# q, k, v of the first attention, rotated keys and latents of the second: from float32 matmuls to three float32r products of high and low parts

## The reference

```
x  = x + layernorm(attention1(layernorm(x)))          # "layer 1"
x1 = layernorm(x)
# attention1: 16 heads of 32
qkv = x @ w_qkv ; q, k = rotary(q), rotary(k)
out = softmax(causal(q k^T / sqrt(32))) v @ w_o
# "layer 2": latent attention on rmsnorm(x1) * ln1_w, then x = x + layernorm(h + experts(h))
kv_d = x @ kv_d_w ; q_d = x @ q_d_w                   # the latents, 128 wide each
k = [kv_d @ k_u_w, rotary(x @ rope_k_w)]              # plain keys, rotated keys
q = [q_d @ q_u_w, rotary(q_d @ rope_q_w)] ; v = kv_d @ v_u_w
h = x1 + softmax(causal(q k^T / sqrt(32))) v @ o_w
```

## Time and profile before

| | |
|---|---|
| median of three runs | 2467.84 us (2466.0 to 2468.34) |
| the profiled execution, its own time | 2468.37 us |
| its span in the trace | 2466.6 us |
| TensorE busy | 2212.0 us, 90% |
| VectorE / ScalarE / GpSimd busy | 61% / 44% / 43% |
| granted TensorE clock, mean | 0.956 |
| attention part (64 head groups) | from the start to about 1715 us |

### The profile page before, as it was taken

The page is one execution under the profiler, slowest core; times in us unless marked ns, Lnnn a source line. Parts: engine busy times, 40 slices in busy tenths (PEclk is TensorE's granted clock), DMA queues, the critical chain, the costliest instruction groups (busy, mean ns, idle before and its releaser), DMA issues. The chain is left out here.

```text
span 2466.6 us, 38146 instructions
## 1 busy us (share of the span) xinstructions
PE 2212.0 (90%) x12944; PEld 1515.4 (61%) x12944; DVE 1511.5 (61%) x4192; ACT 1083.1 (44%) x2214; POOL 1064.4 (43%) x1092
## 2 busy tenths in 40 slices
PE   6898989989898998988899898898498899999994
PEld 5665555656555566655656665464266688888873
DVE  3656667665676765667666566765366556655657
ACT  1334554333555433454533344454233255555543
POOL 1455454444554443456353355544145233333322
PEclk9999999999999999999999999997699899999996
DMA  5443545434455443444544444343438588788796
GB/s 176 113 121 103 145 141 161 121 111 113 121 146 167 122 134 104 119 131 139 163 121 127 129 115 132 98 106 103 169 129 290 209 217 198 184 214 200 185 274 228
DMA packets 221391, 374.83 MB, mean 152 GB/s; under 512 B 24847, under 2 KB 95375, under 8 KB 218383
## 3 DMA queue, kind: packets, MB, share of 16 engines
q1 hardware_dynamic: 157454, 272.69, 37.8%
q0 software_dynamic: 17792, 39.99, 8.4%
q10 hardware_dynamic: 45952, 59.71, 6.7%
HBM read 126.88 MB, written 144.24 MB: 110 GB/s over the span
## 5 line engine op out<-in xcount | busy, mean ns | idle before, releaser
L646 ACT ACTIVATE probs<-scoresT 128x512 f32<-128x512 f32 (+3 forms) x1024 | 417.8, 436 | 551.5 <-PE scoresT L1031 545.9
L827 DVE CUSTOM_DVE_ANT_0 unused<-score,mask 128x128 bf16<-128x128 f32 (+3 forms) x1024 | 465.8, 485 | 267.9 <-PE score L1008 254.0
L1008 PE MATMUL score<-stacks 96*128 96x256 f32 (+2 forms) x1024 | 390.6, 425 | 49.7 <-DVE rowmax L827 47.9
L1031 PE MATMUL scoresT<-stacks 97*128 97x256 f32 (+2 forms) x1024 | 406.2, 432 | 22.0 <-ACT probs L646 10.1
L579 POOL TENSOR_TENSOR probs<-probs 128x1536 f32<-128x1536 f32 (+1 forms) x128 | 373.2, 2916 | 46.4 <-PE out_ps L1045 38.4
L1008 PEld LDWEIGHTS score<-stacks 96*128 96x128 f32 x1024 | 182.3, 193 | 250.6 <-issue 179.9
L840 DVE RECIPROCAL total<-total 128x128 f32<-128x128 f32 x256 | 232.7, 932 | 95.4 <-ACT whole L657 90.0
L568 POOL TENSOR_SCALAR_AFFINE_SELECT probs<-probs 128x512 f32<-128x512 f32 x256 | 164.2, 641 | 291.7 <-ACT probs L646 291.6
L938 PE MATMUL middle<-wqkv,XT 128*128 128x128 f32 x2048 | 270.1, 280 | 7.1 <-ACT XT L613 6.1
L938 PEld LDWEIGHTS middle<-wqkv,XT 128*128 128x128 f32 x2048 | 260.4, 195 | 22.1 <-issue 8.4
L1668 POOL DMA_INDIRECT h_summed<-y,goal x88 | 141.7, 1610 | 292.3 <-ACT y L1764 272.2
(11 more groups left out here) (185 smaller groups left out, 3815.0 us busy)
## 6 DMA issues: line engine op xcount, KB each, us to landing
stacks<-parts SPq DMA_DIRECT2D x768, 128.0 KB, 2.4
x_slots<-mask ACTq DMA_DIRECT2D x56, 1032.0 KB, 4.7
xr<-x_slots SPq DMA_DIRECT2D x22, 1032.0 KB
raw<-in_gates SPq DMA_DIRECT2D x24, 512.0 KB
raw<-in_ups SPq DMA_DIRECT2D x24, 512.0 KB
raw<-in_downs SPq DMA_DIRECT2D x24, 512.0 KB
normed<-in_L_attn_x SPq DMA_DIRECT2D x8, 1024.0 KB, 8.7
rows<-in_L_attn_x SPq DMA_DIRECT2D x8, 1024.0 KB, 5.6
```

What stands on the lines that cost most here:

```text
L646: act.activation(probs[j][:, h, 0:width], scoresT[:, u % ST_BANKS, first:first + width], ACT.Exp, scale=SCALE).then_inc(exp_done, 1)
L827: ins = dve.tensor_tensor_reduce(unused[:, t, 0:width], score.bank(name)[:, first:first + width], mask[:, T - width:T], 1.0, MASKED, ALU.a ...
L1008: ins = pe.matmul(score.bank(name)[:, first:first + width], heads[0:ROWMAX, 0, h, t * P:(t + 1) * P], heads[0:ROWMAX, 1, h, 0:width], star ...
L1031: pe.matmul(scoresT[:, u % ST_BANKS, 0:T - first], heads[0:ROWMAX + 1, 1, h, j * P:(j + 1) * P], heads[0:ROWMAX + 1, 0, h, first:T], start ...
```

## The change

Every operand of P (layer 1), V (layer 1), KR and LAT is split into a high part (float32r, a copy by ScalarE) and a low part (what is left, by VectorE). Instead of one float32 matmul, `three` sums high by high, high by low and low by high, each a float32r matmul. To have 256 moving columns, P makes q and k of a head group side by side: step P(n, 0) is row tiles 0 and 1 of both, P(n, 1) row tiles 2 and 3. So both transposes, of q and of k, now wait for both rotations. V comes in four parts (two row tiles by half of the columns), KR in two (two row tiles, all heads).

The weights are split once at the start (steps WQ, WV for layer 1, WS for layer 2); the raw weights are put into buffers not yet in use. The buffer `wturn` holds the split weights of V for layer 1 or of KR and LAT for layer 2: both versions, 2 MB each, are stored to DRAM (WK) and read back when the layer turns (WT, seven times). `wo` holds one layer's weights and is loaded again at each turn (WO). The input of an attention, transposed, is `xh` and `xl`: its PSUM bank is free only after VectorE has written `xl`.

V parts 2 and 3 of an attention are made in its own g = 1, parts 0 and 1 in g = 2 and 3 of the one before. KR stands wholly in g = 2. `columns_of` is adapted, with XT at four times its columns; `S_AT` starts at 0.27 instead of 0.24.

The diff, cut:

```
-S_AT = (0.24, 0.055)
+S_AT = (0.27, 0.055)
...
     if g == 1:
+        early = quarters("V", c, 2) + quarters("V", c, 3)
+        if starts and start_layer == 1 and core_of(c)[1] == 0:
+            early += [("WT", p)]
...
-            steps = own[:4] + quarters("Y", f, 3) + own[4:] + [("HS", f)]
+            steps = early + quarters("Y", f, 3) + own + [("HS", f)]
...
     if step == "P":
-        return (4 * CT * P, 4 * P)[core_of(which[0] // NG)[1]]
+        return (12 * P, 4 * P)[core_of(which[0] // NG)[1]]
...
     if step == "XT":
-        return 2 * T
+        return 8 * T
...
-                *(("XT", 0, k) for k in range(CT)), *quarters("P", 0, 0), *quarters("P", 0, 1), ("NL", 1),
-                *quarters("P", 1, 0), ("T", 0, 0), ("T", 0, 1), *quarters("P", 1, 1), *quarters("V", 0, 0)]
+                *(("WQ", k) for k in range(2 * CT)), *(("XT", 0, k) for k in range(CT)), *quarters("P", 0, 0),
+                *quarters("P", 0, 1), ("NL", 1), *(("WV", k) for k in range(CT)),
+                *quarters("P", 1, 0), ("T", 0, 0), ("T", 0, 1), *quarters("P", 1, 1)]
...
+                def low_columns(p, k):
+                    name = "XT", p, k
+                    dve.wait_ge(x_high, CT * p + k + 1)
+                    dve.scalar_tensor_tensor(out=xl[:, k, :], in0=middle.bank(name),
+                                             scalar=ln1w[:, k:k + 1] if core_of(p)[1] == 1 else 1.0, in1=xh[:, k, :],
+                                             op0=ALU.mult, op1=ALU.subtract).then_inc(middle.release(name), 1)
...
+                def three(to, left, right, first, last):
+
+                    for n, (a, b) in enumerate(((0, 0), (0, 1), (1, 0))):
+                        ins = pe.matmul(to, left[a], right[b], start=(first and n == 0), stop=(last and n == 2))
+                    return ins
...
+                        t = k // 2
+                        to = middle.bank(name)[:, t * 2 * P:(t + 1) * 2 * P]
+                        for c in (k % 2 * 2, k % 2 * 2 + 1):
+                            mine = [wqk[:, m, c, :].rearrange("p (w d) -> p w d", w=2)[:, :, g * P:(g + 1) * P] for m in range(2)]
+                            ins = three(to, rows_by_part(c, 2 * which + t), mine, c == 0, c == CT - 1)
...
                     pe.wait_ge(*middle.empty(name))
                     pe.wait_ge(rotated[which], n + 1)
+                    if core_of(n // NG)[1] == 0:
+                        pe.wait_ge(rotated[1 - which], n + 1)
```

More of the change, by code:

```diff
@@ L114, in projections_between @@
         steps = rows_of_group(n + 2)
+        if c == 0:
+            steps += [("WS", k) for k in range(CT)] + [("WK",)]
         if ends:
@@ L148, in projections_between @@
     if g == 2:
-        steps = [("XT", p, k) for k in range(CT)] if starts else []
+        steps = [("WO", c)] + [("XT", p, k) for k in range(CT)] if starts else []
         if starts and start_layer == 1:
-            steps += quarters("KR", n + 4) + quarters("LAT", p, 1) + quarters("P", n + 4, 0)
+            steps += quarters("KR", p, 0) + quarters("LAT", p, 1) + quarters("KR", p, 1) + quarters("P", n + 4, 0)
             steps += quarters("LAT", p, 0) + quarters("KU", n + 4)
@@ L164, in projections_between @@
         steps += rows_of_group(n + 5)
-        for t in range(2 * (1 - start_layer), TT):
-            steps += quarters("V", p, t)
+        for part in range(1 - start_layer, 2):
+            steps += quarters("V", p, part)
     return steps
@@ L178, in columns_of @@
     if step == "V":
-        return 4 * T if core_of(which[0])[1] == 0 else T
-    if step in ("Y", "LAT"):
+        return 12 * P if core_of(which[0])[1] == 0 else 4 * P
+    if step == "LAT":
+        return 3 * T
+    if step == "Y":
         return 4 * T
@@ L263, in middle_fills @@
             yield ("q", "k")[which[1]], which[0]
-        if step in ("KR", "KU") and which[1] == 0:
+        if step == "KU" and which[1] == 0:
             yield step, which[0]
-        if step in ("V", "Y", "LAT") and which[2] == 0:
+        if step in ("V", "Y", "LAT", "KR") and which[2] == 0:
             yield step, *which[:2]
@@ L487, in _ @@
                         load_rows(*which)
+                    if step == "WK":
+                        keep_parts()
+                    if step == "WT":
+                        load_turn(*which)
+                    if step == "WO" and which[0] >= 2 and which[0] % 2 == 0:
+                        load_wo(*which)
                     if step == "XS":
@@ L726, in _ @@
                     if step == "XT":
[L727 to L728 removed]
+                        columns(*which)
                     if step == "LAT" and which[2] == 3:
@@ L918, in latents, with project @@
                         pe.wait_ge(*middle.empty(name))
-                    ins = pe.matmul(middle.bank(name), wlat[:, c, m, :], xT[:, c, :], start=(c == 0), stop=(c == CT - 1))
+                    ins = three(middle.bank(name), [wturn[:, n, c, LATENTS[m]] for n in range(2)], (xh[:, c, :], xl[:, c, :]),
+                                c == 0, c == CT - 1)
                     if c == CT - 1:
                         ins.then_inc(middle.filled, 1)
-                def project(n, which, t):
+                def project(n, which, k):
```

337 lines of the change are left out of this document (221 added, 116 removed).

## The result

The changed kernel takes 2446.8 us (median of 4 runs, 2445.2 to 2453.1) against 2467.0 for the kernel before: a ratio of 0.9922 (95% interval 0.9904 to 0.9941), 20 us less. The forecast was 2388 us, with a range of 2350 to 2440. The profiled execution has a span of 2443.1 us against 2466.6. Two later jobs gave 0.9929 and 0.9915.

The account below looks back on a forecast made before the run. TensorE's matmuls were taken to bound most head groups. From the profiled 2468.4 us, terms -87.5 - 3 - 13 + 6 + 4 + 5 + 6 + 2 = -80.5 gave 2388 us, range 2350 to 2440.

Parts of the forecast that it names:

- The matmuls themselves: Term: P, V, KR and LAT as three float32r products each save TensorE time, -87.5 us together.
- most groups are as long as their matmuls: Opening step: TensorE is busy nearly all of most head groups, such as 28.54 of 29.2 us in group 16.
- the other engines become the bound: Rival: groups fall to a floor above TensorE's need and half the saving stays, 2435 us; chance 0.14.
- V into g=1: Term: two V parts, 5.7 us, move into g=1, whose 5.2 us of waits absorb some: -3 us.
- The normalization: Term: moving it ahead of the first maxima removes a GpSimd stall, 4.6 us in each of three places: -13 us.
- The start: Term: weight splits and XT's low parts delay the prologue, with the first P at 25.3 us: +6 us.
- The transposes of q: Term: they now wait for both rotations in the eight g=1 of layer 1, 0.45 us each: +4 us.
- None elsewhere: Sign: a wait of about 3 us before q's transposes in g=1 of layer 1, and in no other groups.
- XT: Term: VectorE writes one more low part per bank, 0.747 us, 64 times: +5 us, upper case 22.
- no net cost: Claim that KR moving wholly from g=0 to g=2 of the attention before, on the same engine, costs nothing.
- DMAs: Term: the 4 MB store in group 0 and the later 2 MB reloads on SyncE's queue cost +2 us.
- Less filling: Term: as filling work shrinks, waits for exponentials and maxima show in the groups: +6 us.

Follow-up runs that it names:

- e1: Changed kernel with two products instead of three in every split projection, so the output lacks a correction: 2352.7 us, ratio 0.9605.
- e14: e12 with two products instead of three in every split projection, so the output lacks a correction: 2340.2 us, ratio 0.9479.
- e12: Changed kernel with e2's later reload, XT at 12T for layer 2 inputs, e9's V order and 12 idle transposes before KR: 2384.5 us, ratio 0.9742.
- e13: Kernel before, with only the four normalizations moved to the front of g=1, ahead of the first maxima: 2449.2 us, ratio 0.9929.
- e9: Changed kernel with the V steps in g=1 no longer all at the front, four taking places of fillers: 2407.8 us, ratio 0.9838.
- e7: Changed kernel with idle transposes on TensorE, 12 before the first KR product and 24 before q's transposes, four and eight places apart: 2438.8 us, ratio 0.9897.
- e3: Changed kernel with XT counted as 2T columns instead of 8T, so its four steps stand in one piece: 2479.5 us, ratio 1.0127.
- e2: Changed kernel with the 2 MB reload of layer 1's V weights moved from g=3 of the third attention to g=1 of the fourth: 2409.9 us, ratio 0.9843.
- e10: Changed kernel without the splits of layer 2's weights and their half of the store, so layer 2's numbers are wrong: 2426.1 us, ratio 0.9906.
- e8: Changed kernel with the V weight splits behind the first transposes and P of head group 1: 2445.9 us, ratio 0.9927.
- e4: Changed kernel with a group's first maxima at 0.24 of its columns instead of 0.27: 2429.0 us, ratio 0.9933.

## Why the prediction was wrong

By its own steps:

- **The matmuls themselves (-87.5).** The sizes were right, 0.118 and 0.23 us. What failed is the step above it, "so most groups are as long as their matmuls", by which the saving was priced in full: e1 and e14 show that of work taken from TensorE 69% and 57% arrive in the time, and e12 against e13 that 46 of the 87.5 us could be had (0.9742 against 0.9929, both without the stall). The rest became idle time and a slower clock. It is near the rival "the other engines become the bound" (half of the saving stays, 2435 us), to which I gave 0.14 and which came nearest of all cases; but that rival had no term for the clock nor for the placements, so its nearness to 2446.8 is in part luck. Group 27 with 17.0 us was read as a proof that groups can become short; for groups that hold P, V and KR it was no bound at all.
- **V into g=1 (-3 for what its waits absorb).** Wrong in sign for g=1 of c mod 4 = 1, where the group grew by 4.2 us, all of the work that came in (48 x 0.118 for V less 1.4 for P), while TensorE's idle time stayed (28.75 - 23.71 = 5.0 us before, 33.17 - 27.72 = 5.5 after, in group 21). e9 shows that the place at the front cost 21 us in all. For c mod 4 = 0 e13 settles it: 24.1 us without the stall and without V, 28.7 with V. Nothing was absorbed there either; the 5.2 us of waits of group 17 that I meant to fill were 2.9 of stall, gone by itself, and a wait at the transposes.
- **The normalization (-13).** Right, and 5 us too small: -17.7 alone (e13). I had left out the place in attention 0.
- **The start (+6).** First P at 26.63 us instead of 25.3; ScalarE began its splits at 16.79, behind 1.28 us that it spends on a table load, an instruction that the rows of before had not shown me there. But the sum counted that 11 us of products leave the prologue, and the prologue did not shorten (59.9 before, 59.6 to 62.2 after), where 6 of the 11 were to be eaten by the later start: the first P runs at half clock until 30.4 us, behind waits of 7.3 and 1.7 us for low columns.

```profile
15.49 1.28 ACT L678 ACT_TABLE_LOAD   x1 [15.49 <-DMA probs<-in_L_attn_w_qkv]
16.79 4.27 ACT L678 ACTIVATE wqk<-qk 128x512 fp32r<-128x512 f32 x8
...
23.01 1.97 PE L1039 MATMUL middle<-ident,normed 128*128 128x128 f32 x8 [7.29 <-DVE xl L912]
26.63 0.76 PE L1046 MATMUL middle<-wqk,xh 128*128 128x256 f32 x2 [1.66 <-DVE xl L912]
```

- **The transposes of q (+4).** Half right: the wait grew by 0.4 in group 17 (2.7 us), but fell in group 21, from 4.0 to 2.4, where waits for maxima now stand ahead of it. "None elsewhere" failed: g=1 of c mod 4 = 3 has a new wait of 1.6 us.
- **XT (+5) and KR "no net cost".** The g=2 groups with layer 2's keys grew by 3.0 us. By their products alone (KR and LAT, 48 x 0.118 + 24 x 0.23 after, 32 x 0.111 + 16 x 0.429 before) they should have grown by 0.8, and in e12 they grew by 1.0 and 1.3. The group that half of KR left, 2, g=0, should have shortened by 32 x 0.111 = 3.6 and gave 2.7. So most of what KR and LAT were to save, 22 us in eight attentions, did not arrive. The waits for lows sum to 20 us in the head groups, 2.4 to 2.7 in each of these eight, where the prediction took +5 and had 22 as its upper case; but the waits for ScalarE's copies of XT, 20 us before in all g=2 groups, are gone, so as idle time XT costs nothing more. What was not in the sum is that the waits now stand together and that the clock falls behind them: e7 gets 1.4 to 1.7 us back in each of eight such groups, and e3 shows how steep the price is (+51) when XT stands closer.
- **DMAs (+2).** The step that failed is "the reloads start at a group's front, and need less than a group". This reload is issued 10 us into group 27, the short one of 17.6 us, with two loads of 1 MB beside it. Measured: 14 us in the groups, 19 in the time (e2). The splits and the store in group 0 cost up to 4 (e10).
- **Less filling (+6).** Not measured apart. Layer 2's g=3 groups, which gave 1.7 us of work away, grew from 17.2 and 17.4 to 17.8 and 18.4, and TensorE's idle time there from 0.4 and 0.6 to 2.1: they gave nothing back.
- **Half-clock time** stood in no term but the stall's. In the records of the head groups 99 us lie at the lower level before, 145 to 162 in the three profiles of the changed kernel, 104 in e9, 83 in e12. Each is worth at most half of itself, so some 25 us of the missing 57 (80.5 - 23.5, the difference of the spans of the two profiles); it overlaps the waits that it follows, and is no term beside them.

Added up, by ratios: moving the normalization takes 17.5 us off the kernel before (e13). From there to e12, where the placements are mended, are another 46. The changed kernel lies 44 above e12: the reload 19 (e2), V's place 21 (e9), XT and the clock behind it some 4. -17.5 - 46 + 44 are the 19 us gained. Against the forecast, the products and all smaller terms brought 46 instead of 67.5 (87.5 + 3 less 23 for start, transposes, XT, filling and DMAs), the placements cost 44 where the sum had next to nothing, and the stall gave 4.5 more: 21.5 + 44 - 4.5 are the 61 us that are missing. The parts of the 44 are not independent (e9's 21 us contain time at the lower clock that e7 gets back in another way), and how the 21.5 divide between the other engines' chains, the clock and the prologue (5) was not measured apart.

## What to carry to other kernels

A kernel whose main engine is busy 98% of a group is not bound by it alone: before pricing a saving in full, leave some of the engine's work out in a trial run and see what share of it arrives. Moved work was paid in full where it landed, and again by its place at the front of the stage; put it in the places of the fillers. What a busy engine is spared can come back as a slower clock: count the time at either clock before and after. A load that is hidden by size is not hidden if it is issued in the shortest stage beside two others: look for the smallest DMA with the nearest deadline, on any queue.

## What the runs showed of the hardware

- A DMA on one queue is held up by large ones on another: the negated maxima on ScalarE's queue landed after 9.4 us instead of 1.8 with 4 MB issued on SyncE's 8 us before; with 2 MB fewer there (e2) TensorE's wait for it fell from 6.7 to 1.0 us.
- TensorE's granted clock fell to 1.2 GHz behind short single waits in otherwise full groups: in group 21 at 634.6 us, 0.9 us behind a wait of 1.75, and in group 22 at 651.7, 0.6 us behind one of 1.4; 7.4 of group 22's 33.7 us are at 1.2 GHz. The same wait doesn't always do it: with 1.6 us at the transposes group 29 has a mean clock of 0.96, group 45 of 1.00. 12 idle transposes in the wait for the lows left 3.2 of 6.4 us at 1.2 GHz (g=2 of c mod 4 = 2, e7).
- In some jobs ScalarE stands still in the expert part, between two instructions, for up to 10.6 us at a time (e8, e13), and the profile names nothing of the kernel as releaser. The waits of ScalarE in the changed kernel's first profile:

```profile
ACT xh L1897 <- remote: 17.0, 5, 5.7
ACT acts L1929 <- remote: 15.1, 3, 7.2
ACT zT L1902 <- remote: 9.7, 1, 9.7
```

  The profiles of e1 to e4 and e9 to e12 have no such row, and the part behind the head groups was 15 to 18 us shorter in them; the kernel before took 17 us less in these jobs too. One chip showed it in one job and not in the other. What it is stays open.
